# Cross attention that mixes unnormalised probabilities with the tokens on partitions, and scores by halves of the rows

## The reference

```python
# x: after the first residual; ctx_512: (8, 256, 128), is both k and v
N_HEADS, N_GROUPS, HEAD_DIM = 16, 4, 32          # 4 heads of a group share keys and values
qh = q.reshape(b, s, N_GROUPS, 4, HEAD_DIM).transpose(0, 2, 3, 1, 4)    # q = layernorm(x)
kh = k.reshape(b, s, N_GROUPS, HEAD_DIM).transpose(0, 2, 1, 3)
vh = v.reshape(b, s, N_GROUPS, HEAD_DIM).transpose(0, 2, 1, 3)
scores = jnp.einsum('bghsd,bgtd->bghst', qh, kh) / math.sqrt(HEAD_DIM)
probs = jax.nn.softmax(scores, axis=-1)
out = jnp.einsum('bghst,bgtd->bghsd', probs, vh)
return out.transpose(0, 3, 1, 2, 4).reshape(b, s, 512) @ Wc.T + bc
```

## Time and profile before

| | us |
|---|---|
| median of 3 runs | 2391.81 |
| profiled execution | 2389.02 |
| span in its trace | 2387.3 |
| PE busy | 2091.1 (88%) |
| DVE busy | 1800.4 (75%) |
| ACT busy | 1598.1 (67%) |
| GpSimd busy | 710.7 (30%) |
| L1522, scores, 256 records | 130.6 |
| L1662, normalising, 256 records | 109.3 |

### The profile page before, as it was taken

One profiled execution on the slowest core, in us unless ns is written; L12 is line 12 of the kernel. 1 busy time (PEld: TensorE's weight loads), 2 busy tenths in 40 slices (PEclk: granted clock), 3 DMA queues, 4 the chain that ended last, 5 costly groups with the idle time before them and its releaser, 6 DMA issues. The chain is left out here.

```text
span 2387.3 us, 56010 instructions
## 1 busy us (share of the span) xinstructions
PE 2091.1 (88%) x19136; PEld 1521.8 (64%) x19160; DVE 1800.4 (75%) x4181; ACT 1598.1 (67%) x4506; POOL 710.7 (30%) x610
## 2 busy tenths in 40 slices
PE   5699899899899899899899899858999999756998
PEld 2477677677677677677677677645666666424444
DVE  8677777777777777777777777636888888764997
ACT  2577777777777777777777777636767777633343
POOL 7212112112112112112112112113566666550332
PEclk8799999999999999999999999779999999977999
DMA  2100000100100100100100100052333323113111
GB/s 73 50 9 24 30 9 22 32 9 22 32 9 22 32 9 22 32 9 22 32 9 22 32 9 22 19 181 83 95 98 97 97 90 90 41 45 120 56 55 51
DMA packets 122930, 108.16 MB, mean 45 GB/s; under 512 B 12080, under 2 KB 97072, under 8 KB 122800
## 3 DMA queue, kind: packets, MB, share of 16 engines
q1 hardware_dynamic: 122800, 106.87, 14.3%
HBM read 72.24 MB, written 34.60 MB: 45 GB/s over the span
## 5 line engine op out<-in xcount | busy, mean ns | idle before, releaser
L588 PE MATMUL proj<-xn_hi,w_lo 128*128 x768 | 367.0, 478 | 0.0
L589 PE MATMUL proj<-xn_lo,w_hi 128*128 x768 | 309.6, 403 | 0.0
L590 PE MATMUL proj<-xn_hi,w_hi 128*128 x768 | 309.5, 403 | 0.0
L968 DVE SCALAR_TENSOR_TENSOR qkv<-conv_in,taps,qkv 128x512 f32<-128x512 f32 x384 | 295.2, 789 | 0.0
L1189 POOL TENSOR_TENSOR o_scale<-o_var,neg_half 128x4 f32<-128x4 f32 x68 | 67.7, 1012 | 577.0 <-DVE o_var L989 577.0
L1205 POOL TENSOR_TENSOR k_len<-sumsq,pos_half 128x4 f32<-128x4 f32 x32 | 47.1, 1473 | 636.3 <-DVE sumsq L1136 636.3
L1080 DVE TENSOR_TENSOR i_less_r<-bank_c,join_mask 128x256 f16<-128x256 f32 x330 | 124.6, 418 | 133.5 <-PE bank_c L652 132.4
L887 ACT ACTIVATE inv<-bank_b 128x256 f16<-128x256 f32 x330 | 110.8, 381 | 162.9 <-PE bank_b L673 159.5
L590 PEld LDWEIGHTS proj<-xn_hi,w_hi 128*128 128x128 f32 x768 | 147.5, 192 | 35.2
L588 PEld LDWEIGHTS proj<-xn_hi,w_lo 128*128 128x128 f32 x768 | 146.6, 191 | 26.1
L834 ACT ACTIVATE g_mask<-mask_ge,g_cols 128x128 fp32r<-128x128 f32 x528 | 158.0, 407 | 0.0
(11 more groups left out here) (287 smaller groups left out, 5924.5 us busy)
## 6 DMA issues: line engine op xcount, KB each, us to landing
out_t<-o_out SPq DMA_DIRECT2D x68, 256.0 KB, 2.0
o_raw<-out_t SPq DMA_DIRECT2D x32, 512.0 KB, 5.4
w_raw<-in_L_attn_W_qkv_dram SPq DMA_DIRECT2D x36, 256.0 KB, 2.8
wq_dram<-wq_q SPq DMA_DIRECT2D x48, 128.0 KB, 1.9
w_raw<-in_L_attn_W_z_dram SPq DMA_DIRECT2D x18, 256.0 KB, 2.7
x_sb<-in_x_dram SPq DMA_DIRECT2D x16, 256.0 KB, 2.7
x_in<-in_x_dram SPq DMA_DIRECT2D x16, 256.0 KB, 5.7
wq_raw<-in_L_ffn_w_gate_dram SPq DMA_DIRECT2D x16, 256.0 KB, 2.6
```

Of the source, the lines that this page charges most:

```text
L588: pe.matmul(out, w_lo[:, k, cols], sh.xn_hi[:, k, tok], start=(k == 0), stop=False)
L589: pe.matmul(out, w_hi[:, k, cols], sh.xn_lo[:, k, tok], start=False, stop=False)
L590: product = pe.matmul(out, w_hi[:, k, cols], sh.xn_hi[:, k, tok], start=False, stop=(k == KT - 1))
L968: dve.scalar_tensor_tensor(out=out, in0=conv_in[:, j, :, k:k + T], scalar=taps[:, j, k:k + 1], in1=out, op0=ALU.mult, op1=ALU.add).then_in ...
```

## The change

The matmuls of `scores` take the 64 rows of the two heads that they compute. The probabilities are not normalised before they are turned; `normalise` is gone, and `turn_probs` waits for the exponentials. `turned` is two copies on ACT, none on DVE. In `mix` the turned probabilities are stationary and the values move, so tokens are on partitions and `ps_v[u]` is laid out by head. The sums of all 16 heads are kept, `reciprocals` runs once a batch and tile (in group 3), `weighted` on DVE scales the whole mix into `mix_t`, and `turn_mix` on PE transposes it back into `ps_v[u]`. `mixed` reads it from there.

```diff
--- before.py
+++ after.py
@@ -1270,8 +1270,10 @@
         rstd = [sb(f"rstd1_{u}", [P, 1], F32) for u in U]
         neg_max = [sb(f"neg_max{u}", [P, PER], F32) for u in U]
         shift = [sb(f"shift{u}", [P, PER], F32) for u in U]
-        sums = [sb(f"sums{u}", [P, PER], F32) for u in U]
-        r_sums = [sb(f"r_sums{u}", [P, PER], F32) for u in U]
+        sums = [sb(f"sums{u}", [P, HEADS], F32) for u in U]
+        r_sums = [sb(f"r_sums{u}", [P, HEADS], F32) for u in U]
+        mix_both = sb("mix_t", [P, 2, D], F32)
+        mix_t = [mix_both[:, u, :] for u in U]
         probs = [sb(f"probs{u}", [P, PER, T], F32) for u in U]
         probs_t = [sb(f"probs_t{u}", [P, 2, PER, P], F32) for u in U]
         mix_hi = [sb(f"mix_hi{u}", [P, KT, P], F32R) for u in U]
@@ -1294,12 +1296,12 @@
 
 
         wo_raw = ([probs[u][:, :, :].rearrange("p (o j) t -> p o (j t)", o=2) for u in U]
-                  + [sb("wo_raw", [P, 2, D], F32)[:, :, :], k_rep[:, :, :, :, :].rearrange("p k c j d -> p k (c j d)")])
+                  + [mix_both[:, :, :], k_rep[:, :, :, :, :].rearrange("p k c j d -> p k (c j d)")])
         WP = KO // 2
         wc_raw = [probs_t[u][:, :, :, :].rearrange("p o j t -> p o (j t)") for u in U]
         wc_t = x2
         ps_s = [[st.enter_context(nc.psum_tensor(f"ps_s{u}{i}", [P, 2 * T], F32)) for i in range(2)] for u in U]
-        ps_v = [st.enter_context(nc.psum_tensor(f"ps_v{u}", [P, KT, P], F32)) for u in U]
+        ps_v = [st.enter_context(nc.psum_tensor(f"ps_v{u}", [P, D], F32)) for u in U]
         ps_y = st.enter_context(nc.psum_tensor("ps_y", [P, D], F32))
         ps_t = st.enter_context(nc.psum_tensor("ps_c", [P, D], F32))
 
@@ -1315,8 +1317,9 @@
                                                                  two("rstd1_done"), two("xn1_done"))
         t_ps, q_done, s_ps, max_done, shift_done, exp_done = (two("t1_ps"), two("q_done"), two("s_ps"), two("max_done"),
                                                               two("shift_done"), two("exp_done"))
-        rs_done, norm_done, pt_ps, pt0_done, pt1_done, pv_ps = (two("rs_done"), two("norm_done"), two("pt_ps"),
-                                                                two("pt0_done"), two("pt1_done"), two("pv_ps"))
+        rs_done, mt_done, mt_ps, pt_ps, pt0_done, pt1_done, pv_ps = (two("rs_done"), two("mt_done"), two("mt_ps"),
+                                                                     two("pt_ps"), two("pt0_done"), two("pt1_done"),
+                                                                     two("pv_ps"))
         mhi_done, mlo_done, c_ps, x2_done, x2_dma = (two("mhi_done"), two("mlo_done"), two("c_ps"), two("x2_done"),
                                                      two("x2_dma"))
         q_var_done, q_rstd_done, xm_done, x_blocks, xy_done, x8_done, xq_done, xq_dma = (
@@ -1519,12 +1522,13 @@
                     pe.wait_ge(pt0_done[u], GROUPS * b + c)
                     pe.wait_ge(pt1_done[u], GROUPS * b + c)
                     for i in range(2):
-                        last = pe.matmul(ps_s[u][i][:, :], q_t[u][:, c, :], k_blocks[:, c, 2 * i:2 * i + 2, :],
+                        pair = slice(2 * HD * i, 2 * HD * i + 2 * HD)
+                        last = pe.matmul(ps_s[u][i][:, :], q_t[u][pair, c, :], k_blocks[pair, c, 2 * i:2 * i + 2, :],
                                          start=True, stop=True)
                     last.then_inc(s_ps[u], 1)
 
                 def turn_probs(b, c, u):
-                    pe.wait_ge(norm_done[u], GROUPS * b + c + 1)
+                    pe.wait_ge(exp_done[u], GROUPS * b + c + 1)
                     for k in range(2):
                         for j in range(PER):
                             last = pe.transpose(ps_s[u][k][:, P * j:P * j + P], probs[u][:, j, P * k:P * k + P], ident[:, :])
@@ -1534,12 +1538,20 @@
                     if c == 0:
                         pe.wait_ge(mlo_done[u], b)
                         pe.wait_ge(ctx_v_in, 16 * (b + 1))
-                    for k in range(2):
-                        pe.wait_ge((pt0_done, pt1_done)[k][u], GROUPS * b + c + 1)
-                        for j in range(PER):
-                            last = pe.matmul(ps_v[u][HD * j:HD * j + HD, c, :], ctx_v[:, k, HD * c:HD * c + HD],
-                                             probs_t[u][:, k, j, :], start=(k == 0), stop=(k == 1))
+                    pe.wait_ge(pt0_done[u], GROUPS * b + c + 1)
+                    pe.wait_ge(pt1_done[u], GROUPS * b + c + 1)
+                    for j in range(PER):
+                        for k in range(2):
+                            at = HD * (PER * c + j)
+                            last = pe.matmul(ps_v[u][:, at:at + HD], probs_t[u][:, k, j, :], ctx_v[:, k, HD * c:HD * c + HD],
+                                             start=(k == 0), stop=(k == 1))
                     last.then_inc(pv_ps[u], 1)
+
+                def turn_mix(b, u):
+                    pe.wait_ge(mt_done[u], b + 1)
+                    for k in range(KT):
+                        last = pe.transpose(ps_v[u][:, P * k:P * k + P], mix_t[u][:, P * k:P * k + P], ident[:, :])
+                    last.then_inc(mt_ps[u], 1)
 
                 def combine(b, u):
                     pe.wait_ge(mlo_done[u], b + 1)
@@ -1576,6 +1588,8 @@
                                     project(b + 1, piece, piece + 1)
                                 elif piece >= PIECES and further:
                                     project(b + 2, piece - PIECES, piece - PIECES + 1)
+                            if before and c == 0:
+                                turn_mix(b - 1, u)
                             if before or c + u:
                                 mix(*last_tile(b, c, u))
                             if before:
@@ -1613,6 +1627,7 @@
                 turn_probs(B - 1, GROUPS - 1, 1)
                 mix(B - 1, GROUPS - 1, 1)
                 for u in U:
+                    turn_mix(B - 1, u)
                     combine(B - 1, u)
 
             @block.scalar
@@ -1651,27 +1666,26 @@
                 def weigh(b, c, u):
                     act.wait_ge(shift_done[u], GROUPS * b + c + 1)
                     act.wait_ge(pt_ps[u], GROUPS * b + c)
+                    if c == 0:
+                        act.wait_ge(rs_done[u], b)
                     for j in range(PER):
                         last = act.activation(probs[u][:, j, :], ps_s[u][j // 2][:, T * (j % 2):T * (j % 2) + T], ACT.Exp,
-                                              bias=shift[u][:, j:j + 1], scale=SCALE, accum_out=sums[u][:, j:j + 1])
+                                              bias=shift[u][:, j:j + 1], scale=SCALE,
+                                              accum_out=sums[u][:, PER * c + j:PER * c + j + 1])
                     last.then_inc(exp_done[u], 1)
-
-                def normalise(b, c, u):
-                    act.wait_ge(rs_done[u], GROUPS * b + c + 1)
-                    for j in range(PER):
-                        last = act.activation(probs[u][:, j, :], probs[u][:, j, :], ACT.Copy, scale=r_sums[u][:, j:j + 1])
-                    last.then_inc(norm_done[u], 1)
 
                 def turned(b, c, u):
                     act.wait_ge(pt_ps[u], GROUPS * b + c + 1)
                     act.wait_ge(pv_ps[u], GROUPS * b + c)
-                    act.activation(probs_t[u][:, 0, :, :].rearrange("p j s -> p (j s)"), ps_s[u][0][:, :],
-                                   ACT.Copy).then_inc(pt0_done[u], 1)
+                    for k, done in enumerate((pt0_done, pt1_done)):
+                        act.activation(probs_t[u][:, k, :, :].rearrange("p j s -> p (j s)"), ps_s[u][k][:, :],
+                                       ACT.Copy).then_inc(done[u], 1)
 
                 def mixed(b, u):
-                    act.wait_ge(pv_ps[u], GROUPS * (b + 1))
+                    act.wait_ge(mt_ps[u], b + 1)
                     act.wait_ge(c_ps[u], b)
-                    act.activation(mix_hi[u][:, :, :], ps_v[u][:, :, :], ACT.Copy).then_inc(mhi_done[u], 1)
+                    act.activation(mix_hi[u][:, :, :], ps_v[u][:, :].rearrange("p (k t) -> p k t", k=KT),
+                                   ACT.Copy).then_inc(mhi_done[u], 1)
 
                 def step(b, before, after, further):
                     for c in range(GROUPS):
@@ -1685,7 +1699,6 @@
                             weigh(b, c, u)
                             if before and (c, u) == (0, 0):
                                 queries(b, 1)
-                            normalise(b, c, u)
                             if before:
                                 if (c, u) == (0, 0):
                                     mixed(b - 1, 0)
@@ -1775,21 +1788,24 @@
                     dve.wait_ge(exp_done[u], GROUPS * b + c)
                     dve.tensor_scalar(shift[u][:, :], neg_max[u][:, :], SCALE, None, ALU.mult).then_inc(shift_done[u], 1)
 
-                def reciprocals(b, c, u):
```

(31 more changed lines are left out.)

## The result

The changed kernel takes 2413.02 us, the median of four runs (2405.97 to 2417.86), against 2391.27 for the kernel before on the same chip: a ratio of 1.009, with the interval 1.006 to 1.0119. It is slower by 22 us, where 11 us less were forecast (2380, range 2364 to 2408). Its profiled execution is its quickest, 2405.97 with a span of 2404.0, so the trace accounts for 16.7 us of the loss. Its two longer runs (2416.37 and 2417.86) have a mean granted clock of 0.936 and 0.937, the two shorter ones 0.942 and 0.941.

What follows compares the result with a forecast made beforehand. PE with gaps was taken to bound six of eight batches, waits the last. Six batches gave -6.6 and the last -5, so -11.6 from the median 2391.81: 2380 us, range 2364 to 2408.

Steps and rivals of the forecast that it cites:

- The scores: Scores call on PE: two 64-row halves overlap fully, so 1.71 us falls by half, a gain of 0.86 a slot.
- The Trainium skill's share: Scores call: the skill page's measured speedup of 3.07 for four row tiles would give 1.1 us, time about 2397.
- rival 1: Scores: row halves do not overlap, +55 us to 2435 (chance 0.10), or overlap in one pass, +27 to 2407 (0.05).
- The mix: Mix on PE with probabilities stationary: 16 records at 0.112, 1.79 us, or +1.35 a slot.
- the turn of the mix: New turn_mix on PE: four transposes for each of two tiles, 0.45 us each, +0.9 a batch.
- PE's work of a batch: PE in a middle batch: scores, mix and new turn add 4.8 us to 55.8, making 60.6.
- The batch of 62.2: Middle batch: 60.6 us of PE work plus 1.6 of waits, against 63.3; -6.6 over six batches.
- the 55.8 of work: Kernel before: PE's own work in a 63.3 us batch summed to 55.8, the remaining 7.5 being waits.
- What is late next: Slot-by-slot waits left: DVE enters (0,0) 3.3 late, delivers at 5.4 against PE's 5.0, wait 0.5 with the signal.
- rival 2: DVE's queue behind two 2.5 us reciprocals in (3,0), (3,1) keeps waits at 4.5 a batch; 2398 us, chance 0.13.
- Waits left: 1.6: Middle batch: PE's remaining waits after the change total 1.6 us.
- The last batch: Last batch: ordinary slots at 5.0 to 5.2 and less normalising gain, the end adds 3 to 4; sum -5 us.

Runs made afterwards that it cites:

- ordered: Changed kernel with four moves: reciprocals later, multiplication ahead of maxima, queries' copy ahead of exponentials on ACT, both end turns ahead of both combines; 2386.22 us.
- late_sums: Changed kernel with a tile's reciprocals moved from slot (3, u) to slot (0, u) of the next batch, before the multiplication; 2400.1 us, ratio 1.0034.
- filled_wait: Changed kernel with sixteen unused transposes of the identity on PE ahead of the mix's turn in slot (0, 0); 2400.37 us, ratio 1.0046.
- ordered_filled: Changed kernel with four moves of order, plus unused transposes filling PE's gaps in the last batch; 2377.38 us, ratio 0.9941.
- rows_only: Kernel before with only the new scores by row halves, mix and normalising as they were; 2385.75 us, ratio 0.9985.
- rows_no_norm: Kernel before with row halves in the scores and without reciprocals and normalising, the division left out altogether; 2350.21 us, ratio 0.9813.
- before_filled: Kernel before with eight unused transposes ahead of and behind the turn in each last-batch slot, three more groups at the end; 2388.44 us, ratio 0.9982.

## Why the prediction was wrong

Right, by its own steps:

- The scores. 0.86 was taken, 1.06 measured, from 1.71: the halves overlap, but not in full. The prediction had left the cost of entering and leaving the tile shape out of both sides, and took 0.44 for the old mix, which costs 0.57. So scores and mix together were priced at +0.49 a slot and measured 1.23 - 0.65 = +0.58: 0.09 a slot too low, 6 us of PE's work in 64 slots. The Trainium skill's share ("TensorE: Matmul & The Clock Gate", Part 3, Measured speedup) gave 1.1 in the prediction's estimate, and the trace agrees with it better than with a full half. Neither form of rival 1 came (1.71, or 1.29).
- The mix, 1.79 against 1.80 and 1.71; the turn of the mix, 0.45 against 0.43 to 0.49 at full clock; PE's work of a batch, 60.6 against 61.5 (the 63.5 of batch 4 less its wait).
- The waits of the earlier trace rows for normalising, for `q_t` and for DVE's copy are gone from the list.
- The batch of 62.2 was right for the work, as `ordered` shows, but not for the order in which the change puts it. That it is right to a tenth is luck: in `ordered` it is 61.3 of work and 1.0 of waits, where 60.6 and 1.6 were priced. The start was off in the same way: the 55.8 of work stood beside 57.4 busy in the earlier trace rows, and the waits that the trace lists in that batch are 5.9, not 7.5.

Wrong:

- "What is late next", (0, 0): "Wait 0.5 with the signal". It was 1.99. PE asked for it at 5.3, near the 5.0 priced; DVE gave it at 7.3 and not at 5.4. The step took DVE's lag as 3.3 us on entering (0, 0), and it was 4.35 (1869.65 to 1874.00), and took maxima and shift as 1.45, and they took 2.23. The mechanism was named, the reciprocal that holds DVE 2.5 us with everything behind it, and the size was off: `xn` took 1.50 there and the operations on four and sixteen columns about 1.0 each, the stretched durations that the earlier trace rows showed once (1.02). `late_sums` settles that the reciprocal is at the root of it; that the others are stretched by GpSimd's work beside them is read from the traces, and not tested. This is rival 2's place and mechanism, which had 0.13; but its price, waits of 4.5 us a batch, was not what made it dear: the waits of a middle batch are 2.3 (11.5 us in five).
- "Waits left: 1.6" was taken as the whole price of waiting. No term priced the granted clock in batches 1 to 6. Several waits of up to 1.8 us (batches 2 to 5) became one of 2.0, and that one lets the clock fall in some executions of the batch, which costs 3 us where it falls for 6.8. `filled_wait` shows it: same lateness, no fall, 12.6 us less by the medians, 10.5 by the ratios.
- "The last batch", sum -5; it was +12.1. "5.0 to 5.2" a slot is nearly right at full clock (5.29), and three of four slots ran at 6.9, for which the sum had no term. The earlier trace rows had the warning, a clock of 0.83 in that stretch: the change puts work onto TensorE just where its granted clock is low, and it went down to 0.72. The first three slots, with the late multiplications, lost 5.7 (PE waits 3.33 at the turn in (0, 0)), and the end 5.2 in place of 3 to 4. In that end the second tile's turn stands behind the first combine, so that `finish` of tile 0 waits for it on DVE:

```profile
2144.04 0.60 PE L1553 MATMUL ps_v<-ident,mix_t 128*128 128x128 f32 x4
2148.00 0.47 PE L1565 MATMUL ps_c<-wc_hi,mix_lo 128*128 128x512 f32 x1 [3.36 <-DVE x L1814]
```

  The prediction saw the order, and priced the copies behind it, but not that the second combine needs the bank which `finish` has to empty, and that this one stands behind mix_lo of tile 1 and a piece of the weights' quantising in DVE's queue.

In sum, what failed is the wait at the turn in (0, 0), 0.5 for 1.99, and a clock that no term priced, in the middle and above all in the last batch. Put into the best order found and with the clock held up, as in `ordered_filled`, batches 1 to 6 take 4.5 us less than before and the last batch 4.8 less, where 6.6 and 5 were priced. That is near, though the filling adds work that the prediction did not know.

What the prediction never asked is whether the swap of the mix is a good trade. `rows_only` shows that PE's waits in the kernel before belong to a chain, and grow when PE gets quicker. `rows_no_norm` shows what taking the reciprocals and the normalising out of it is worth, 3 to 4 us in a batch from 2 to 6 and 8 in the last, against 8 x 1.23 + 0.9 = 10.7 us of PE's work for the mix and its turn.

## What to carry to other kernels

Before a chain is shortened by work on TensorE, price that work at the clock that the stretch really grants, and look at the slots in which the engine has nothing else to do. When several short waits are removed, work out the longest one that is left: a single wait of 2 us cost here more than its length. An in-order queue is the first thing to look at when an operation is moved to one slot of a period: what it waits for there, it makes all that is queued behind it wait for, and four moves of order were worth 27 us, more than the change cost. Where an operation takes longer in one place than elsewhere, look at what the other engines run at its start and at its end.

## What the runs showed of the hardware

- Two fp32 matmuls of 64 rows and 512 columns, each on its own half of the rows and into its own bank, take 1.06 us together, where two of 128 rows take 1.71 to 1.82 at full clock.
- The granted clock fell to 0.50 behind a PE wait of 1.99 us, in some batches and not in others, and with the wait filled by sixteen transposes it did not fall. That rests on one profiled execution of each, and on the medians. It also fell for 3.4 us in a few batches of `late_sums` and `ordered`, where the waits listed between 1743 and 2040 us are 0.8 us at most; what sets that off is open.
- Transposes that compute nothing, put in PE's gaps, made the program faster: by 9 us in `ordered_filled` against `ordered`, by 12.6 us in `filled_wait` against the changed kernel (8 and 10.5 by the ratios). In `before_filled` the gain, 4 us, could not be placed.
- DVE operations on 128 x 4 and 128 x 16 elements, 0.17 us as a rule, took 0.99 to 1.05 in the crowded stretch between slots (3, 1) and (0, 1). All 46 of the stage that took over 0.25 us began while a GpSimd operation ran and ended within 0.06 us behind the end of one. That is a reading of the trace; no run changed GpSimd's work.
